# Last attention unit of an adaLN block on one Trainium2 core: own buffers for its second half, other orders, gate rows written in unit 1, and filler matmuls on TensorE

## What is computed

```
mod = (silu(c) @ wmod).reshape(16, 6, 1, 128)
sa, ca, ga, sb, cb, gb = mod[:, 0] ... mod[:, 5]      # ga, gb: magnitude at least 0.25
h = layernorm(x) * (1 + ca) + sa
x = x + ga * attention(h)          # linear attention, 16 heads, second-order Taylor features
h = layernorm(x) * (1 + cb) + sb
x = x + gb * ffn(h)
# ffn: p = softmax(h @ Ws + bs); each of 8 experts takes the 512 tokens with its highest p
#      out = gelu(h @ W1 + b1) @ W2 + b2, times p, added to the token's row
```

## Time and profile before

| | |
|---|---|
| median of the runs (three) | 350.55 us |
| the profiled execution, its own time | 347.35 us |
| its span, first to last instruction | 345.6 us |
| mean granted TensorE clock, of full speed | 0.864 |
| busy: TensorE, VectorE, ScalarE, GpSimd | 71%, 61%, 47%, 51% |
| attention units | up to about 177.7 us |
| rest of the last unit, to the last logits | about 177.7 to 195.6 us |
| softmax and transpositions of it | 195.6 to 203.9 us |
| counting and slots | 203.9 to 242.9 us |
| experts, gathers, scatters | 234.9 to 345.6 us |

### The profile page before, as it was taken

The page is one execution under the profiler, slowest core; times in us unless marked ns, Lnnn a source line. Parts: engine busy times, 40 slices in busy tenths (PEclk is TensorE's granted clock), DMA queues, the critical chain, the costliest instruction groups (busy, mean ns, idle before and its releaser), DMA issues.

```text
span 345.6 us, 8069 instructions
## 1 busy us (share of the span) xinstructions
PE 245.1 (71%) x3056; PEld 173.1 (50%) x3056; DVE 210.2 (61%) x675; ACT 162.8 (47%) x223; POOL 177.3 (51%) x221
## 2 busy tenths in 40 slices
PE   1679999999999999999873341140899986769300
PEld 1346666767676676767652240030377754636300
DVE  5162898989999898987986668869232222122200
ACT  6265869685885968688530166400433333033000
POOL 5517437274663727451524200006767887876666
PEclk9998999999999999999985565555699999898855
DMA  6707101010110101010010799982333344333233
GB/s 192 206 3 293 78 17 48 17 33 17 33 32 15 46 15 30 18 47 18 17 48 16 95 91 100 339 168 70 108 82 55 56 78 59 52 77 31 23 30 30
DMA packets 30542, 24.06 MB, mean 70 GB/s; under 512 B 6368, under 2 KB 27184, under 8 KB 30128
## 3 DMA queue, kind: packets, MB, share of 16 engines
q0 software_dynamic: 6848, 9.06, 18.8%
q1 hardware_dynamic: 23664, 14.59, 14.1%
HBM read 15.11 MB, written 8.54 MB: 68 GB/s over the span
## 4 chain that ended last, share of the span: by engine, by line
DVE 33%; PE 22%; POOL 19%; issue 13%; ACT 8%; DMA 3%; DVEq 1%; POOLq 0%; ACTq 0%
POOL out_y L570 10%; PE ps L1347 5%; PE ps L1357 4%; POOL rstd L481 3%; ACT area L703 3%; DVE y_s L785 3%; DMA out_y<-o_sb,idx 3%; PE ps L1145 3%; DVE low L1058 3%; DVE y_n L790 2%; DVE wgt L760 2%; DVE xn L825 2%; DVE area L750 2%; POOL area L560 2%; PE ps L1175 2%
## 5 line engine op out<-in xcount | busy, mean ns | idle before, releaser
L634 ACT ACTIVATE wgt<-ps 128x1024 f32<-128x1024 f32 x64 | 62.3, 1027 | 37.2 <-PE ps L1145 37.2
L570 POOL DMA_INDIRECT out_y<-o_sb,idx x32 | 50.5, 1578 | 17.7 <-issue 8.5
L560 POOL DMA_INDIRECT area<-token_rows,idx x32 | 31.0, 969 | 52.1 <-DVE idx L1071 42.7
L1145 PEld LDWEIGHTS ps<-area 32*128 32x128 f32 x1024 | 42.1, 184 | 25.4 <-ACT wgt L644 13.2
L1145 PE MATMUL ps<-area 32*128 32x64 f32 (+3 forms) x1024 | 50.3, 321 | 3.3 <-ACT wgt L634 1.2
L1175 PE MATMUL ps<-wgt,v_bd 128*32 128x259 f32 (+3 forms) x1024 | 43.6, 312 | 2.9 <-DVE y_t L776 2.1
L714 ACT ACTIVATE area<-ps,b_sb 128x512 f32<-128x512 f32 x32 | 21.9, 687 | 49.6 <-PE ps L1347 49.6
L1175 PEld LDWEIGHTS ps<-wgt,v_bd 128*32 128x32 f32 x1024 | 29.9, 112 | 14.4 <-DVE y_t L776 3.3
L1357 PE MATMUL ps<-modb,area 128*128 128x128 f32 x256 | 33.1, 292 | 2.1 <-ACT area L714 2.1
L1357 PEld LDWEIGHTS ps<-modb,area 128*128 128x128 f32 x256 | 32.0, 207 | 3.9 <-ACT area L714 3.9
L1347 PE MATMUL ps<-area,xall 128*128 128x512 f32 x64 | 31.0, 629 | 1.0 <-DVE area L1077 1.0
(11 more groups left out here) (181 smaller groups left out, 442.1 us busy)
## 6 DMA issues: line engine op xcount, KB each, us to landing
modb<-mod_rows SPq DMA_DIRECT2D x3, 1024.0 KB, 7.5
out_y<-x SPq DMA_DIRECT2D x16, 128.0 KB, 1.8
token_rows<-h SPq DMA_DIRECT2D x16, 128.0 KB, 1.9
token_rows<-gb_mod POOLq DMA_DIRECT2D x1, 2048.0 KB, 28.2
xall<-in_w SPq DMA_DIRECT2D x1, 2048.0 KB, 29.2
modb<-in_w SPq DMA_DIRECT2D x8, 256.0 KB, 6.4
xall<-in_x SPq DMA_DIRECT2D x2, 768.0 KB, 8.7
xall<-in_x SPq DMA_DIRECT2D x2, 256.0 KB, 5.1
```

The source lines that it names most:

```text
L560: eng.indirect_dma_start(out=xg[e % 4][:, j, :], out_offset=None, in_=rows[:, :], in_offset=bass.IndirectOffsetOnAxis(ap=idx[:, e, j:j + 1 ...
L570: eng.indirect_dma_start(out=out[:, :], out_offset=bass.IndirectOffsetOnAxis(ap=idx[:, e, j:j + 1].bitcast(u32), axis=0), in_=o_sb[e % 2][ ...
L634: k = nc.scalar.activation(wgt[bb][:, 2 * half:2 * half + 2, :, 0:256], ps[:, 2 * half:2 * half + 2, :].rearrange("p c (a q) -> p c a q", ...
L1145: return mm(ps[:, cc, col:col + SEQ - key * BK], k_bd[par][qd][r, 4 * bb + key, :, :].rearrange("p a k -> p (a k)"), q_sb[par][qd][r, t0 + ...
```

## The change

Six things, all at the end of the attention:

- The second half of the last unit gets buffers and semaphores of its own (`last_stats`, `last_mom`, `last_vare`, `last_rstd`, `last_xn2`, `last_h2_t`).
- VectorE: the `digits` go from before the last unit's rest to behind `last_modulate`; `logits(v - 1, 1)` goes in front of `y_norm(v, 0)`; the last half's moments go in front of `normalise2(v, 0)`.
- GpSimd: the last half's reciprocal root goes in front of `modulate2(v, 0)`; the DMA of the gate rows goes to the end of unit 1.
- ScalarE issues the DMA of `pr_te` instead of SyncE, behind its copy into `pr_te`.
- TensorE: both halves are transposed before both are routed.
- TensorE: `keep_warm(n)` issues n matmuls whose result nobody reads, 128x128 by 128x256 in float32 into PSUM bank 1; 35 of them in all, in batches that wait for the steps of the other engines.

```diff
+        last_stats = sb("last_stats", [P, 2, 6], fp32)
+        last_mom = sb("last_mom", [P, 2, 2], fp32)
+        last_vare = sb("last_vare", [P, 2], fp32)
+        last_rstd = sb("last_rstd", [P, 2], fp32)
+        last_xn2 = sb("last_xn2", [P, 2, D], fp32)
+        last_h2_t = sb("last_h2_t", [P, SEQ], fp32)
...
+        s_stl = sem("last_stats_ready")
+        s_mol = sem("last_moments_ready")
+        s_vel = sem("last_var_eps")
+        s_rsl = sem("last_rstd_ready")
+        s_xnl = sem("last_xn2_ready")
+        s_h2pl = sem("last_h2_t_psum")
+        s_h2tl = sem("last_h2_t_ready")
...
@@ -401,9 +414,6 @@
             eng.dma_start(w1_sb, w1.rearrange("e p f -> p e f")).then_inc(s_wf, 16)
             for e in range(NE):
                 eng.dma_start(w2_sb[:, e, :, :], w2[e, :, :].rearrange("(k p) d -> p k d", p=P)).then_inc(s_wf, 16)
-            eng.wait_ge(s_pte, 1)
-            with nc.allow_non_contiguous_dma(reason="eight probabilities a token"):
-                eng.dma_start(rows[:, 2 * D:ROW].rearrange("(t p) e -> p t e", p=P), pr_te[:, :, :]).then_inc(s_pro, 16)
...
@@ -539,18 +549,20 @@
                     modulate2(v, 1)
                 if not (isinstance(u, int) and u >= UNITS - 2):
                     rstd1_of(u + 2, par)
+                if isinstance(u, int) and u == 1:
+                    eng.wait_ge(s_gbk, 1)
+                    eng.dma_start(rows[:, D:2 * D].rearrange("(b n) d -> b n d", b=NB),
+                                  gb_mod[:, :].unsqueeze(1).broadcast_to([NB, SEQ, D])).then_inc(s_gbrow, 16)
 
             units(eng, unit)
             v = UNITS - 1
             residual_add(v, 0)
             rstd2_of(v, 0)
+            eng.wait_ge(s_mol, 1)
+            nc.gpsimd.tensor_scalar(last_vare[:, :], last_mom[:, :, 1], EPS_LN, None, ALU.add).then_inc(s_vel, 1)
+            eng.wait_ge(s_vel, 1)
+            nc.gpsimd.tensor_tensor(last_rstd[:, :], last_vare[:, :], half_neg[:, 0:2], ALU.pow).then_inc(s_rsl, 1)
             modulate2(v, 0)
-            rstd2_of(v, 1)
-
-            eng.wait_ge(s_gbk, 1)
-            eng.dma_start(rows[:, D:2 * D].rearrange("(b n) d -> b n d", b=NB),
-                          gb_mod[:, :].unsqueeze(1).broadcast_to([NB, SEQ, D])).then_inc(s_gbrow, 16)
...
@@ -684,7 +696,8 @@
             units(eng, unit)
             h2_copy(UNITS - 2, 1)
             h2_copy(UNITS - 1, 0)
-            h2_copy(UNITS - 1, 1, T_BANK)
+            eng.wait_ge(s_h2pl, 1)
+            nc.scalar.activation(last_h2_t[:, :], ps[:, T_BANK, 0:SEQ], ACT.Copy).then_inc(s_h2tl, 1)
...
@@ -693,6 +706,9 @@
                                  pr[:, :, NT // 2:NT].rearrange("p e t -> p t e").unsqueeze(3)
                                  .broadcast_to([P, NT // 2, NE, NC]), ACT.Copy).then_inc(s_rep[1], 1)
             nc.scalar.activation(pr_te[:, :, :].rearrange("p t e -> p e t"), pr[:, :, :], ACT.Copy).then_inc(s_pte, 1)
+            eng.wait_ge(s_pte, 1)
+            with nc.allow_non_contiguous_dma(reason="eight probabilities a token"):
+                eng.dma_start(rows[:, 2 * D:ROW].rearrange("(t p) e -> p t e", p=P), pr_te[:, :, :]).then_inc(s_pro, 16)
             for n in range(2, 4):
                 eng.wait_ge(s_ptp, n + 1)
                 nc.scalar.activation(p_all[:, 512 * n:512 * n + 512], ps[:, n, :], ACT.Copy).then_inc(s_pall, 1)
...
@@ -837,8 +853,8 @@
 
                 b = 2 * v + 1
                 eng.wait_ge(s_h2o[1], 16 * v + 16)
-                eng.wait_ge(s_xn2, 2 * v + 2)
-                nc.vector.tensor_tensor(y_n2, xn2[:, :, :], cb_sb[:, b:b + 1, :].broadcast_to([P, 2, D]), ALU.mult)\
+                eng.wait_ge(s_xnl, 1)
+                nc.vector.tensor_tensor(y_n2, last_xn2[:, :, :], cb_sb[:, b:b + 1, :].broadcast_to([P, 2, D]), ALU.mult)\
...
@@ -941,25 +957,37 @@
 
             units(eng, unit)
 
-            eng.wait_ge(s_cb, 2)
-            for n, shift in enumerate(SHIFTS):
-                k = nc.vector.tensor_scalar(digits[:, n:n + 1], part_i[:, :], NC - 1, shift, ALU.bitwise_and,
-                                        ALU.logical_shift_left)
-            k.then_inc(s_bs, 1)
             v = UNITS - 1
             y_out(4 * v + 2, 0, 1)
+            logits(v - 1, 1)
             y_norm(v, 0)
-            logits(v - 1, 1)
             y_out(4 * v + 3, 1, 1)
             gate(v, 0)
             y_norm(v, 1)
             moments2(v, 0)
             gate(v, 1, T_BANK)
             last_residual(v)
+            eng.wait_ge(s_x1l, 1)
+            for t in range(2):
+                k = nc.vector.bn_stats(last_stats[:, t, :], x1[1][:, t, :])
+            k.then_inc(s_stl, 1)
+            eng.wait_ge(s_stl, 1)
+            alone(eng)
+            for t in range(2):
+                k = nc.vector.bn_aggr(last_mom[:, t, :], last_stats[:, t, :])
+            k.then_inc(s_mol, 1)
             normalise2(v, 0)
-            moments2(v, 1, True)
-            normalise2(v, 1)
+            eng.wait_ge(s_rsl, 1)
+            for t in range(2):
+                k = nc.vector.tensor_scalar(last_xn2[:, t, :], x1[1][:, t, :], last_mom[:, t, 0:1], last_rstd[:, t:t + 1],
+                                            ALU.subtract, ALU.mult)
+            k.then_inc(s_xnl, 1)
             last_modulate(v)
+            eng.wait_ge(s_cb, 2)
+            for n, shift in enumerate(SHIFTS):
+                k = nc.vector.tensor_scalar(digits[:, n:n + 1], part_i[:, :], NC - 1, shift, ALU.bitwise_and,
+                                        ALU.logical_shift_left)
+            k.then_inc(s_bs, 1)
             logits(v, 0)
             logits(v, 1, T_BANK)
...
@@ -1201,14 +1229,25 @@
                 bank = T_BANK if last and bb else B_PO
                 for t in range(2):
                     k = tr(ps[:, bank, t * P:(t + 1) * P], h2[bb][:, t, :], ident[:, :])
-                k.then_inc(s_h2p, 1)
+                k.then_inc(s_h2pl if last and bb else s_h2p, 1)
 
             def route(v, bb, bank=B_PO):
-                eng.wait_ge(s_h2t, 2 * v + bb + 1)
+                last = bank == T_BANK
+                if last:
+                    eng.wait_ge(s_h2tl, 1)
+                else:
+                    eng.wait_ge(s_h2t, 2 * v + bb + 1)
+                h_now = last_h2_t if last else h2_t
                 for t in range(2):
-                    k = mm(ps[:, bank, SEQ + t * NE:SEQ + (t + 1) * NE], h2_t[:, t * P:(t + 1) * P], ws_sb[:, :],
+                    k = mm(ps[:, bank, SEQ + t * NE:SEQ + (t + 1) * NE], h_now[:, t * P:(t + 1) * P], ws_sb[:, :],
                            start=True, stop=True)
                 k.then_inc(s_lgp, 1)
+
+            def keep_warm(n):
+
+                for i in range(n):
+                    mm(ps[:, 1, 0:2 * P], wqk_sb[:, 0, :], wqk_sb[:, 0:2, :].rearrange("p g m -> p (g m)"),
+                       start=True, stop=True)
...
@@ -1275,11 +1314,44 @@
             weighted(v, 1, 1, 1)
             project_out(v, 0)
             eng.wait_ge(s_sq, 6 * UNITS)
+            eng.wait_ge(s_ga, 2 * v + 1)
+            keep_warm(3)
+            eng.wait_ge(s_ys, 2 * v + 2)
+            keep_warm(1)
+            eng.wait_ge(s_rec, 2 * v + 2)
+            keep_warm(2)
+            eng.wait_ge(s_yn, 2 * v + 2)
+            keep_warm(1)
             project_out(v, 1, T_BANK)
+            keep_warm(1)
+            eng.wait_ge(s_ga, 2 * v + 2)
+            keep_warm(1)
+            eng.wait_ge(s_x1l, 1)
+            keep_warm(3)
+            eng.wait_ge(s_mol, 1)
+            keep_warm(4)
+            eng.wait_ge(s_rsl, 1)
+            keep_warm(2)
+            eng.wait_ge(s_xnl, 1)
+            keep_warm(3)
             to_h2_t(v, 0, True)
+            to_h2_t(v, 1, True)
             route(v, 0)
-            to_h2_t(v, 1, True)
             route(v, 1, T_BANK)
+            eng.wait_ge(s_lg, 2 * UNITS + 1)
+            keep_warm(2)
+            eng.wait_ge(s_r, 1)
+            keep_warm(1)
+            eng.wait_ge(s_sh, 1)
+            keep_warm(4)
+            eng.wait_ge(s_ex, 1)
+            keep_warm(2)
+            eng.wait_ge(s_r, 2)
+            keep_warm(1)
+            eng.wait_ge(s_r, 3)
+            keep_warm(1)
+            eng.wait_ge(s_pr, 1)
+            keep_warm(3)
 
             eng.wait_ge(s_pr, 1)
             for i in range(NT // 2):
```

## The result

The changed kernel takes **360.1 us** (median of 4 runs, 359.12 to 362.47), the kernel before on the same chip 350.5 us: ratio **1.0277 [1.0253, 1.0302]**. The forecast was 352.2 us, 349.0 to 354.6. The sign was right by luck: the forecast had the last unit 1.4 us longer, and it became 0.9 us shorter. The loss came from a place that the forecast had at 0.2 us.

A forecast was written before the change was run, and what follows sets the result against it. The prediction took the chain of single steps from the last attention unit to GpSimd's first scatter as the bound, with no engine full. Last unit +1.4 and DMAs +0.2 on 350.55 gave 352.2 us, range 349.0 to 354.6.

The forecast's parts named there:

- DMAs: Gate rows' DMA in unit 1: nearly hidden, 0.2 us lost (0 to 1.7); ScalarE's issue of `pr_te` costs nothing.
- Seven before the second projection: Last unit: seven small matmuls, at half clock until about 186.5, start the projection at 187.5 instead of 185.01; loss 2.5 us.
- Price: Cost of one `keep_warm` matmul on TensorE: 0.43 us at full clock, 0.86 at half; bounds 0.43 and 0.59.
- The rival with calls under 0.25 us: Small matmuls fit in the waits and the clock stays up: about -4.1 us, 346.4 us; chance 0.15.
- Twelve before the transpositions: Last unit: 12 small matmuls take 5.2 us behind `x1`, so transpositions start at 194.4, 1.2 us later than before.
- pay nothing while the small matmuls stand: Last unit: new order and moved DMA gain nothing because TensorE's queue ends last, 194.4 against 193.05 for the arithmetic.
- The hold of 1.0 us by the DMA issue: Last unit's second normalise took 1.65 us, held by GpSimd's gate-row issue; moving that DMA removes 1.0 us.
- Fourteen in the softmax: 14 small matmuls take 6.0 us; the 16 transpositions then take 1.8 us at full clock instead of 3.65; 1.6 gained.
- rival 2: Small matmuls too long, but the clock comes back at once or never falls: -0.5+0.2, 350.25 us; chance 0.15.
- ScalarE's issue of `pr_te`: Issue moved from SyncE, where it took 0.77 us: costs nothing; if it takes 3.68, ScalarE comes 1.1 us late.
- Rival 3: ScalarE's queue is held by its DMA, delaying critical copies and sign counts some 20 us: 370 us; chance 0.05.
- Sum: Whole kernel: +1.4 for the last unit and +0.2 for DMAs, about +1.6 on 350.55, giving 352.2 us.

The follow-up runs named there:

- e1: Changed kernel with the gate rows' DMA back behind GpSimd's last modulate, all else as changed: 346.97 us, ratio 0.9994.
- e2: Kernel before the change with only the gate rows' DMA moved to the second unit (unit 1): 358.03 us, ratio 1.0284.
- e4: Changed kernel without small matmuls and with the gate rows' DMA back behind the last modulate (own buffers and orders only): 345.62 us, ratio 0.9958.
- e11: e4 plus seven small matmuls of 256 columns in the softmax, none before it: ratio 0.9926.
- e7: e4 with GpSimd's products of the last unit's first half held until VectorE's last normalise is through: 349.65 us, ratio 0.9964.
- e9: Changed kernel with the gate rows as four 0.5 MB DMAs cut along the tokens, in the first two and last two units: 348.82 us, ratio 1.0043.
- e5: Changed kernel with the gate rows' DMA issued by SyncE, ahead of its first store in the loop over units, instead of GpSimd: 371.39 us, ratio 1.0585.
- e12: Changed kernel with the gate rows as two 1 MB DMAs cut along the tokens, in the second and last unit: 352.11 us, ratio 1.012.
- e13: e4 plus a 2 MB DMA into an unread table, issued twice in the loop over units: 356.65 us, ratio 1.0245.
- e3: Changed kernel without the 35 small matmuls, gate rows' DMA still in unit 1: 357.36 us, ratio 1.0287.
- e8: e1 with the 35 small matmuls cut from 256 to 64 columns: ratio 1.0038.

## Why the prediction was wrong, point by point

- **"DMAs": the gate rows in unit 1 are "nearly hidden", 0.2 us, between 0 and 1.7.** This step failed: the DMA cost 10.4 us (changed kernel against e1; 10.8 by the medians of e2). I priced GpSimd's 1.71 us of issue and a hold on VectorE, and took the 26.9 us on the DMA engines to be free, since TensorE, full in that stretch, moves no data by them. It does: its own instructions, of which one fetch came 10.5 us late.
- **"Seven before the second projection", clock at 0.50 until 186.5, loss 2.5.** Wrong: in the changed order the clock had not fallen yet when the small matmuls came, and they held it. The calls took 3.26 us and the loss against `y_d` was 1.3. I had read the 0.50 of the earlier trace rows as a property of the place. With the changed orders and no small matmuls at all (e4) it is 1.00 up to 184 us. The prediction's own sign of being wrong, a clock at 1.00 by 184, is what came.
- **"Price", 0.43 at full and 0.86 at half clock.** Right: 0.45 (28 records in 6.31) and 0.86 (e11). The rival with calls under 0.25 us is out. The Trainium skill's 0.109 us for 256 columns (TensorE: Matmul & The Clock Gate, Back-to-back issue gap), for one matmul, doesn't describe these calls, which are two records of 0.22 each.
- **"Twelve before the transpositions", "pay nothing while the small matmuls stand".** Half right. The small matmuls ended last, but only 0.5 us behind `h` (ready at 202.21, start 202.68).
- **The hold of 1.0 us by the DMA issue.** It was one of two. Without the DMA the normalise took 1.55 us instead of 1.65, beside GpSimd's product (e7).
- **"Fourteen in the softmax".** Right: 6.31 us, transpositions 1.91 at full clock. The sum of the last unit was rival 2's: -0.5 there, -0.9 measured, where the forecast had +1.4.
- **ScalarE's issue of `pr_te`:** 0.42 us at 209.56 and hidden, as forecast. Rival 3 is out.
- **Sum.** With +10.4 in place of +0.2 and the measured -0.9 in place of +1.4, 350.55+9.5 gives 360.1: what was measured.

## What to carry to other kernels

A DMA is not free where no engine waits for its bytes: it can hold back the fetch of an engine's instructions. Here TensorE bore a fetch some 5 us late. A load of 7.8 us on all engines stayed inside that, loads of 14.7 and 26.9 didn't, and TensorE then stopped in the middle of a group, with no releaser in the profile. Look at the queues of instruction fetches in the DMA records of such a stretch. Cut such a transfer so that each piece is short on every engine (along the repeated dimension, not across source partitions), or put it where no engine at the bound runs new code, a loop's later pass for one. Cutting wasn't free here (e9 1.0043); the place that the kernel before had for it was (e1 0.9994). And filler matmuls have to fit into their waits: a call too many costs its full price, and the clock it holds is worth only what the real matmuls behind it save.

## What the runs showed of the hardware

- **A stop for instructions**: 5.22, 5.39, 5.39, 1.65 and 7.16 us, in five kernels with a DMA of 14.7 us or more on 16 engines while TensorE ran new code (in the sixth, e5, TensorE waited for `y_t` at that time, 19.39 us). Three things show it: the late fetch that ends 1.2 to 1.4 us ahead of TensorE's next matmul in each of them, the length of the load (e9, e12), and the same load without harm in the loop's second pass (e13). In the changed kernel, e2 and e3, TensorE does 125 matmuls and as many weight loads between its two stops. Not shown is what holds the fetch: at 76.1 us it came through although the gate rows filled the engines until 86.3. The Trainium skill (DMA: Bandwidth & Descriptors, Queues, rings and completion order) has each engine turn from queue to queue after a packet. By that alone a fetch would not be expected 10.5 us late; a packet of the gate rows took 0.7 us.
- **Clock**: from 182 to 184 us TensorE was busy for 1.90 us with the 64-column calls, and the granted clock fell (e8); it was busy for 1.74 us with those of 256 columns, and the clock stayed at 1.00 (e1). I had taken a lost clock to be a matter of idle time alone.
- **3.4 us at the entry of the experts are not of the change.** From the first count to the first scatter it took 52.1 to 53.2 us in the profiled executions of the kernel before, of e1 to e4 and of e9 to e13, and 55.8 to 56.0 in the changed kernel and in e5 to e8. The first group ran where the kernel before takes 347.2 to 348.0 us (its profiled execution took 347.35), the second where it takes 350.5 to 350.7. So they go with the chip that a kernel ran on, and the ratios, each taken on one chip, don't hold them. In the second group VectorE waits there 6.1 to 7.4 us for a release that the profile doesn't name (`remote`), in the first never; what it is stays open.
